# A graph network's input stage: norms interleaved with biases on VectorE, three tiles in seven normed by ScalarE

## The reference

```python
def _layernorm(x, axis=-1, eps=1e-05):
    m = jnp.mean(x, axis=axis, keepdims=True)
    v = jnp.var(x, axis=axis, keepdims=True)
    return (x - m) / jnp.sqrt(v + eps)

def _hconv(x, src, dst, ew, w1, b1, w2, b2, g, b):
    h = jax.nn.relu(x @ w1 + b1)
    msg = ew[:, None] * h[src]
    agg = jax.ops.segment_sum(msg, dst, num_segments=x.shape[0])
    h = agg @ w2 + b2
    return jax.nn.relu(_bn(h, g, b))

x = x + _L0_gnn_ref(_layernorm(x, axis=-1), edge_index, edge_weight, ...)
x = x + _L0_ffn_ref(_layernorm(x, axis=-1)[None], ...)[0]
```

## Time and profile before

| | |
|---|---|
| Median of 3 runs | 5430.35 us (5423.59 to 5431.04) |
| The profiled execution | 5421.78 us, of which its span is 5420.2 us |
| `project_input` in that span | from the first load of `x` at 28.3 us to the last store of `h`, issued at 186.4 us |
| The sum of messages after it | first instructions at 191.7 us |
| Mean busy share in the span | PE 77%, PEld 65%, DVE 59%, POOL 70%, ACT 18% |

### The profile page before, as it was taken

The page is one execution under the profiler, slowest core; times in us unless marked ns, Lnnn a source line. Parts: engine busy times, 40 slices in busy tenths (PEclk is TensorE's granted clock), DMA queues, the critical chain, the costliest instruction groups (busy, mean ns, idle before and its releaser), DMA issues. The chain is left out here.

```text
span 5420.2 us, 135489 instructions
## 1 busy us (share of the span) xinstructions
PE 4191.7 (77%) x20451; PEld 3507.4 (65%) x20452; DVE 3213.5 (59%) x9144; ACT 966.8 (18%) x2131; POOL 3789.6 (70%) x3818
## 2 busy tenths in 40 slices
PE   6778787778777874877878787777776672999998
PEld 5566666666666663766666666666665672888886
DVE  6555555555555556555555555555655664666665
ACT  3100000000000003200000000000001652566665
POOL 2577777777777773877777777777775475566665
PEclk9776767776777776877676767777776555999999
DMA  5433333333333332333333333333333453344443
GB/s 154 130 108 108 108 108 108 108 108 108 108 108 108 108 108 57 127 109 108 108 108 108 108 108 108 108 108 108 108 108 81 130 137 111 61 69 69 69 68 61
DMA packets 359801, 560.35 MB, mean 103 GB/s; under 512 B 128849, under 2 KB 253393, under 8 KB 359474
## 3 DMA queue, kind: packets, MB, share of 16 engines
q0 software_dynamic: 191568, 452.77, 31.7%
q1 hardware_dynamic: 134850, 87.49, 5.9%
q10 hardware_dynamic: 33312, 19.33, 1.3%
HBM read 479.80 MB, written 79.41 MB: 103 GB/s over the span
## 5 line engine op out<-in xcount | busy, mean ns | idle before, releaser
L788 POOL DMA_INDIRECT c_messages<-h,c_indices x3038 | 2879.9, 948 | 950.6 <-issue 918.3
L824 PE MATMUL c_partial<-c_onehot,c_messages 128*128 128x128 f32 x12544 | 2759.7, 371 | 851.2 <-DMA c_messages<-h,c_indices 448.0
L824 PEld LDWEIGHTS c_partial<-c_onehot,c_messages 128*128 128x128 f32 x12544 | 2263.1, 260 | 1350.4 <-issue 775.8
L867 DVE TENSOR_TENSOR sums<-sums,c_partial 128x256 f32 x3136 | 1321.0, 421 | 1590.0 <-PE c_partial L824 1531.5
L840 DVE TENSOR_SCALAR c_onehot<-iota,edge_dst,edge_w 128x128 f32<-128x128 f32 x3152 | 1148.2, 365 | 14.4 <-PEq L103 14.3
L750 ACT ACTIVATE c_indices<-edge_src 128x16 int32 (+1 forms) x200 | 42.9, 215 | 3706.6 <-PE c_partial L824 2752.9
L1755 POOL DMA_INDIRECT out<-ffn_result,ffn_table x204 | 326.4, 1600 | 213.9 <-ACT ffn_result L1885 127.4
L1736 POOL DMA_INDIRECT ffn_rows<-tokens,ffn_table x209 | 215.7, 1032 | 71.5 <-issue 57.2
L804 PE MATMUL c_z<-sums,w 128*128 x768 | 260.6, 501 | 0.0
L1398 POOL DMA_INDIRECT table<-rt_entry,rt_slot x196 | 203.8, 1040 | 69.2 <-issue 57.9
L1804 PE MATMUL ffn_ps<-ffn_w_high,ffn_hT_high 128*128 x816 | 246.9, 303 | 0.0
(11 more groups left out here) (186 smaller groups left out, 3600.5 us busy)
## 6 DMA issues: line engine op xcount, KB each, us to landing
c_messages<-h SPq DMA_DIRECT2D x6272, 1.0 KB
c_messages<-h ACTq DMA_DIRECT2D x6272, 1.0 KB
c_messages<-h,c_indices POOLq DMA_INDIRECT x3038, 3.2
pi_x<-in_x SPq DMA_DIRECT2D x14, 896.0 KB
h<-pi_h ACTq DMA_DIRECT2D x14, 896.0 KB
rt_x<-in_x SPq DMA_DIRECT2D x14, 896.0 KB
out<-rt_x SPq DMA_DIRECT2D x14, 896.0 KB
tokens<-rt_tokens SPq DMA_DIRECT2D x14, 896.0 KB
```

The lines of the kernel that those rows point to most:

```text
L788: pool.indirect_dma_start(messages[:, k, :], None, source, bass.IndirectOffsetOnAxis(ap=indices[:, k:k + 1], axis=0)).then_inc(s_message[k ...
L824: last = pe.matmul(partial[:, k % TURN_BANKS, g * P:(g + 1) * P], messages[:, k, g * P:(g + 1) * P], onehot[:, k % TURN_ONEHOTS, :], start ...
L867: dve.tensor_tensor(where, where, partial[:, k % TURN_BANKS, 0:C].rearrange("p (g n) -> p g n", g=CG), ALU.add).then_inc(s_added, 1)
```

## The change

DVE's and ACT's streams of `project_input` are rearranged. PE's, POOL's and SP's streams keep their order and wait on other counts.

- DVE norms only tiles 0 to 3 of a group (`ON_DVE` = 4). The `scale` of tile j of group g+1 stands right behind the bias of tile j of group g, for j = 0 to 3; biases 4 to 6 follow alone. `keep`, which now stands ahead of the first bias, waits for POOL's power, computes `down` = -mean * rstd for ACT and copies the moments to `node_stats`.
- ACT norms tiles 4 to 6 by `Identity(rstd * x + down)`, for group g+1, between the last `copy_out` of group g and the relus of group g-1.
- `normalize(g+2)` follows the last bias of group g. `moments` has two halves now; two gates that stood behind `scale` are gone from there, and three stand ahead of `bn_aggr`.
- SP's load of `x` waits for the norms of both engines.

```diff
+ON_DVE = 4
...
-        moments = sb("moments", [P, G, 2], F32)
+        moments = sb("moments", [P, 2, G, 2], F32)
+        down = sb("down", [P, 2, G], F32)
...
-                    sp.wait_ge(s_xn, (i * 2 + u + 1) * G)
+                    gate(sp, s_xn, (i * 2 + u + 1) * ON_DVE, passed)
+                    gate(sp, s_xn_act, (i * 2 + u + 1) * (G - ON_DVE), passed)
                     sp.dma_start(x[:, u, :, :], x_view[:, bass.ds((i * 2 + u) * G, G), :]).then_inc(s_x[u], 16)
...
+            def keep(g, u):
                 gate(dve, s_rstd, g + 1, passed)
+                dve.scalar_tensor_tensor(down[:, u, :], moments[:, u, :, 0], -1.0, moments[:, u, :, 1],
+                                         ALU.mult, ALU.mult).then_inc(s_down, 1)
                 dve.tensor_copy(t["node_stats"][:, bass.ds(g * (2 * G), 2 * G)],
-                                moments[:].rearrange("p g s -> p (g s)")).then_inc(s_kept, 1)
+                                moments[:, u, :, :].rearrange("p g s -> p (g s)")).then_inc(s_kept, 1)
+
+            def scale(u, j):
+                dve.tensor_scalar(xn[:, u, j, :], x[:, u, j, :], moments[:, u, j, 0:1], moments[:, u, j, 1:2],
+                                  ALU.subtract, ALU.mult).then_inc(s_xn, 1)
...
+            def bias_and_scale(g, u):
+
+                keep(g + 1, 1 - u)
                 for j in range(G):
-                    dve.tensor_scalar(xn[:, u, j, :], x[:, u, j, :], moments[:, j, 0:1], moments[:, j, 1:2],
-                                      ALU.subtract, ALU.mult).then_inc(s_xn, 1)
...
+                    bias(g, u, j)
+                    if j < ON_DVE:
+                        scale(1 - u, j)
...
             with dve.Fori(0, GROUPS // 2 - 1) as i:
-                normalize(i, i * 2 + 1, 1)
-                bias(i * 2, 0)
-                scale(i, i * 2 + 1, 1)
+                bias_and_scale(i * 2, 0)
                 normalize(i + 1, i * 2 + 2, 0)
-                bias(i * 2 + 1, 1)
-                scale(i + 1, i * 2 + 2, 0)
...
+                bias_and_scale(i * 2 + 1, 1)
+                normalize(i + 1, i * 2 + 3, 1)
...
+            def norm(g, u):
+
+                gate(act, s_down, g + 1, passed)
+                for j in range(ON_DVE, G):
+                    act.activation(xn[:, u, j, :], x[:, u, j, :], ACT.Identity, bias=down[:, u, j:j + 1],
+                                   scale=moments[:, u, j, 1:2]).then_inc(s_xn_act, 1)
...
-            def group(i, g, u, former):
+            def group(i, g, u, former, with_norm=True):
 
                 for j in range(G):
                     copy_out(g, j)
+                if with_norm:
+                    norm(g + 1, 1 - u)
                 if former is not None:
```

More of the change, by code:

```diff
@@ L479, in bias @@
-            def bias(g, u):
-                for j in range(G):
-                    n = g * G + j
-                    dve.wait_ge(s_product, G + n + 1)
-                    dve.wait_ge(s_h, n + 1)
-                    dve.tensor_tensor(biased[:, u, j, :], product[:, j % 4, 0:C], b1[:], ALU.add).then_inc(s_biased, 1)
+                                moments[:, u, :, :].rearrange("p g s -> p (g s)")).then_inc(s_kept, 1)
+            def scale(u, j):
+                dve.tensor_scalar(xn[:, u, j, :], x[:, u, j, :], moments[:, u, j, 0:1], moments[:, u, j, 1:2],
+                                  ALU.subtract, ALU.mult).then_inc(s_xn, 1)
@@ L487, in _, with bias @@
+            def bias(g, u, j):
+                n = g * G + j
+                dve.wait_ge(s_product, G + n + 1)
+                dve.wait_ge(s_h, n + 1)
+                dve.tensor_tensor(biased[:, u, j, :], product[:, j % 4, 0:C], b1[:], ALU.add).then_inc(s_biased, 1)
+            def bias_and_scale(g, u):
+                keep(g + 1, 1 - u)
+                for j in range(G):
+                    bias(g, u, j)
+                    if j < ON_DVE:
+                        scale(1 - u, j)
             normalize(0, 0, 0)
-            scale(0, 0, 0)
+            keep(0, 0)
@@ L489, in _ @@
+            for j in range(ON_DVE):
+                scale(0, j)
+            normalize(0, 1, 1)
             with dve.Fori(0, GROUPS // 2 - 1) as i:
-                normalize(i, i * 2 + 1, 1)
-                bias(i * 2, 0)
-                scale(i, i * 2 + 1, 1)
+                bias_and_scale(i * 2, 0)
                 normalize(i + 1, i * 2 + 2, 0)
-                bias(i * 2 + 1, 1)
-                scale(i + 1, i * 2 + 2, 0)
-            normalize(GROUPS // 2 - 1, GROUPS - 1, 1)
-            bias(GROUPS - 2, 0)
@@ L498, in _ @@
-            scale(GROUPS // 2 - 1, GROUPS - 1, 1)
-            bias(GROUPS - 1, 1)
+                bias_and_scale(i * 2 + 1, 1)
+                normalize(i + 1, i * 2 + 3, 1)
+            bias_and_scale(GROUPS - 2, 0)
+            for j in range(G):
+                bias(GROUPS - 1, 1, j)
+            dve.wait_ge(s_kept, GROUPS)
+            dve.wait_ge(s_xn, (GROUPS + 2) * ON_DVE)
         @block.gpsimd
@@ L540, in _ @@
                         n = g * G + j
-                        pe.wait_ge(s_xn, 2 * G + n + 1)
+                        if j < ON_DVE:
+                            pe.wait_ge(s_xn, 2 * ON_DVE + g * ON_DVE + (j + 1))
+                        else:
+                            pe.wait_ge(s_xn_act, 2 * (G - ON_DVE) + g * (G - ON_DVE) + (j - ON_DVE + 1))
                         pe.wait_ge(s_xnT, 3 + g * G + (j - 2 if j > 2 else 0))
@@ L589, in _ @@
                 group(i, i * 2 + 2, 0, i)
-            group(0, GROUPS - 1, 1, GROUPS // 2 - 1)
+            group(0, GROUPS - 1, 1, GROUPS // 2 - 1, with_norm=False)
             gate(act, s_stored[1], (GROUPS // 2 - 1) * 16 + 16, passed)
```

20 lines of the change are left out of this document (13 added, 7 removed).

## The result

The changed kernel takes 5451.18 us (median of 6 runs, 5448.11 to 5455.99); the kernel before, run beside it, 5427.94 us (6 runs, 5422.67 to 5431.04). The ratio is 1.0045, 95% interval 1.0032 to 1.0058: **23.2 us slower**. The profiled execution of after took 5455.99 us, its span is 5454.2; before, 5421.78 and 5420.2.

A forecast was written before the change was run, and what follows sets the result against it. The prediction took the loop of ScalarE and TensorE to bound the stage. ScalarE's norms +10.6, the start -0.7 and TensorE's clock +14.4 summed to +24.3 us, on the median 5454.7 us, range 5434 to 5475.

The forecast's parts named there:

- What bounds the stage: In the steady stage, the loop of ScalarE and TensorE sets the pace; VectorE costs only 7.0 us.
- ScalarE's norms, 0.49 us each, +10.6 us: Three unhidden norms between a group's last copy and the relus add 1.47 us a group, +10.6 us over 12 groups.
- VectorE costs nothing: VectorE's new order, with `keep` ahead of the biases, is early enough for tile 4's product: no cost.
- The 1.8 us to spare: Margin by which VectorE's first bias of a group ends before TensorE's product of tile 4 needs it.
- Start, -0.7 us: In group 1, without relus, VectorE sets the end; its last copy comes at 58.8 instead of 59.50, -0.7 us.
- Loads and gates at nothing: The load of `x`, now waiting for ScalarE's norms, is needed some 12 us later, so costs nothing.
- The clock, one slow tile a group, +14.4 us: TensorE idles 2.9 us before each group's first product, its clock falls, one tile takes 1.2 us more: +14.4 us.
- The clock holds: Rival: TensorE's clock survives the gap and only ScalarE's loop counts, +9.9 us, 5440.2 us; chance 0.20.
- ScalarE's norms cost nothing: Rival: the norms cost ScalarE's loop nothing, only VectorE's relief is seen, -7.7 us, 5422.7 us; chance 0.07.
- the clock stays low: Rival: TensorE's clock stays low through most of each group, six slow tiles, 86 us, 5527 us; chance 0.05.

The follow-up runs named there:

- a4: Kernel before, with three extra Identity instructions on ScalarE between a group's last copy and the relus, VectorE's order untouched: 5450.71 us against 5428.71.
- a2: Changed kernel with ScalarE's three norms moved from behind a group's last copy to between its copies: 5431.20 us against 5428.71 for the kernel before.
- c2: Changed kernel with GpSimd's zeroing held back until behind VectorE's last norm of the group: one run, 5452.85 us against 5425.86 for the kernel before.
- a1: Changed kernel with six unused products filling TensorE's gap in each group from group 2 on: 5442.53 us against 5428.71 for the kernel before.
- a3: Changed kernel with all seven norms on VectorE, each behind a bias, none on ScalarE: 5434.09 us against 5428.71 for the kernel before.
- b2: Changed kernel with GpSimd's zeroing held back until VectorE has copied the moments: one run, 5450.65 us against 5424.27 for the kernel before.
- c1: Changed kernel with ScalarE's relus and norms woven between copies, three biases ahead of `keep`, zeroing behind VectorE's last norm: 5411.52 us against 5425.86 before.
- c3: Kernel before, with GpSimd's zeroing moved behind VectorE's copy of the moments, beside the next group's norms: 5444.19 us against 5425.86.
- b1: Changed kernel with three more Identity instructions behind ScalarE's three norms, six in all: 5483.15 us against 5424.27 for the kernel before.

## Why the prediction was right

The forecast was 5454.7 us, slower with 0.80; the median is 5451.18, inside the range. Against before's median in the same session (5427.94), the sum of +24.3 us meets +23.2. Point by point:

- **What bounds the stage** (the loop of ScalarE and TensorE, VectorE worth only 7 us): right in its working part. a4, which leaves VectorE alone and lengthens that loop, has a loss like the whole one, and its groups at full clock are as long. But the 7 us don't bound what VectorE can cost in the new order: in a2, with the norms out of the loop's way, its wait for POOL keeps the groups at 10.1 us. That VectorE would be next if ScalarE's part were shorter was right.
- **ScalarE's norms, 0.49 us each, +10.6 us:** right. 1.48 us for three, c6 to c0 4.74 (4.71 predicted) and 5.09 at a jump (5.07), and 132.3 us for 12 groups with the clock held (132.2).
- **VectorE costs nothing:** right from group 2 on, where no product waits for a bias. The step that gave `keep` about 0.2 us and the first bias 0.42 failed: from the start of `down` to the end of the bias it takes 1.42 us, 0.8 more, held up by GpSimd's memset. The 1.8 us to spare covered that in the groups.
- **Start, -0.7 us:** wrong for the same reason; it measured -0.05. In group 1 VectorE has nothing to spare, the product of tile 4 waited 1.73 us, and the group's last copy came at 59.45, not 58.8. c2, without the hold-up, has it at 57.86. The 1.44 us of the first copy stood in the earlier trace rows, and the prediction passed over it.
- **Loads and gates at nothing:** nothing in the traces speaks against it; no wait for a load has a row between 54 and 195 us.
- **The clock, one slow tile a group, +14.4 us:** right in kind, and near in size by luck. In the profile it was 2.7 more, 149.3 - 132.2 = 17.1 us, in 8 falls of about 2.1 us and not 12 of 1.2: not every gap brings a fall, and a fall slows two or three tiles. Both factors were wrong, and their product is close. Five of the falls begin 1.2 to 1.4 us after TensorE has gone on and cost 1.7 us each; three begin 2.1 us into the gap and cost 2.7 to 2.9 each. A slow tile takes 82.10 - 79.97 = 2.13 us, where the forecast had 2.30. The medians with and without the fill put the whole at 9.4, give or take 9; 14.4 lies between. The gap was 3.04 to 3.41 us; 2.9 and 3.2 were predicted.
- **The rivals.** "The clock holds" is what a1 shows when the gap is filled: 13.8 us there (interval 9 to 20), where 9.9 was worked out. "ScalarE's norms cost nothing" is rejected by a4, "the clock stays low" by the stretches at 1.00.

In the profiles the stage lost 28.0 us, 3.7 more than the sum (0.7 at the start, 2.7 clock, 0.3 behind the last copy), and the executions differ by 34.2, where 24.3 were forecast. The medians show 23.2. The profiled execution of after was the slowest of its six, and that of before was faster than all six timed beside it. The interval of the medians is 7 us wide to either side, so their agreement with the sum to a microsecond is partly luck.

What stays open: why one gap of 3 us brings the clock down and the next, as long, does not. In the experiments only more or less idle time was tried, not its spacing. Nor can it be said how long a gap is harmless: a3 has gaps of 1.5 to 2.0 us before the first product of a group, as a2 has (and others of 0.5 to 0.8 us), and its clock falls twice while a2's holds.

## What to carry to other kernels

Ask of a wait not how much it totals but what stands behind it when it goes; here each wait of 1 us for a norm ran beside 3.2 us of ScalarE's queue, which ended at almost the same time, and a "free" engine was part of the loop. Work that moves to an engine with idle time belongs into that idle time, between the instructions that wait, and not ahead of a copy that is ready (the same norms gave +23 us in one order, nothing that can be told in another, and -28 with the relus woven in and VectorE's order changed too). Before placing a GpSimd memset, look at what VectorE does at that moment, and look at TensorE's clock whenever an edit makes its idle time longer.

## What the runs showed of the hardware

- VectorE's copy and norm from SBUF to SBUF, begun while a GpSimd memset of 1.59 us runs, last until it is over: 0.16 to 0.18 us becomes 1.29 (after), 0.40 becomes 1.52 (b2). Biases, which read PSUM, keep their 0.42 us beside it (b2), the seven statistics their 2.38 us (c1, where the memset begins 0.25 us after them), and `down` its 0.17 us (after). The norm that began before the memset keeps its 0.41 us (c3).
- TensorE's clock fell at gaps of 3.0 to 3.4 us in 8 of 12 groups (after), at 4.5 to 4.9 us in all 12 (b1), at 1.08 and 2.06 us with 0.69 us of transposes between in 6 (a4), at 1.00 and 1.16 us with one tile's transposes between in 5 (c3), and at gaps of 1.97 and 1.92 us, some 3.5 us behind one of 0.5 or 0.7 us, in 2 (a3). It held through all 12 single gaps of 1.54 to 1.92 us in a2, and in a1, where 0.4 to 0.8 us were left.
- The fall often comes late: in five of the changed kernel's eight it begins 1.2 to 1.4 us after TensorE has gone on.
- Six useless products a group made the changed kernel faster (5442.53 against 5451.18 us, each beside its own runs of before: +13.8 and +23.2).
